# Two masked attention layers with residual layernorm: row stages rewritten, the first attention's ring and sums rearranged

## The chip, the cores and the metric

One core of one Trainium2 chip. The metric is device time in microseconds (us) of one launch. All inputs and outputs lie in HBM; the work that matters is done by TensorE (PE), VectorE (DVE), ScalarE (ACT), GpSimd (POOL) and the DMA queues that SyncE (SP), ACT and POOL issue.

## The reference, cut to what matters

```python
# N = 4096 nodes, 8 heads of 64, 512 features; adj is a 4096 x 4096 0/1 matrix (about 0.4% ones, diagonal set)
x_l     = (x @ W + b).reshape(N, 8, 64)
scores  = alpha_l[:, None, :] * alpha_r[None, :, :]      # alpha: x_l against att_l, att_r, per head
att     = softmax(where(adj > 0, scores, -9e15), axis=1)
x1      = layernorm(x + relu(einsum('ijh,jhc->ihc', att, x_l)))
scores  = einsum('hnd,hmd->hnm', x1 / 8, x2)             # second layer: x1 as queries, x2 as keys
attn    = softmax(where(adj > 0, scores, -9e15), axis=-1)
out     = layernorm(x1 + einsum('hnm,hmd->hnd', attn, v))
```

## The kernel before, in words

The kernel runs five stages one after the other, with a barrier of all engines between two of them.

1. `prepare` transposes the mask into SBUF as 0/1 bytes, computes `x_l` and the alphas, splits the keys `x2` into two fp16 parts, and writes them to scratch tensors in HBM. Its tail computes one shift per head (a bound on the scores, so that the exponential can't overflow) for the first attention, stores it, loads it back, and compares it with a limit. A branch then takes the plain way (`attend_gat`) or, for large bounds, another one (`attend_with_maximum`). For these inputs the plain way is taken.
2. `attend_gat` is the first attention. It has 16 groups (4 chunks of 1024 queries by 4 pairs of heads), and each group goes over 32 tiles of 128 source rows. Per tile and head ACT computes `exp(scale * al_bc + shift)` (line 515, 128x1024), DVE multiplies it by the mask (line 528), and PE multiplies the result by the values: `values`, line 544, 4 fp32 products per tile, each two matmul records. Masked weights live in a ring `w` of 5 tiles. They are also summed over source rows, for the softmax denominators, in one of two ways. The tiles not in `BY_DMA` (20 of 32) go through PE as products with ones (`denominators`, line 553), two tiles at a time (`COUPLES`); the 12 tiles in `BY_DMA` are added by DMAs with an accumulating write that POOL issues (lines 587 and 589, 1 MB each), in two chains into two totals; PE then multiplies both totals by ones after the fourth tile of the next group (`close`). A place of the ring is free again when its values are multiplied and its sum is done; ACT waits for both. The source rows `g_xl` come in blocks of 4 tiles into 2 places (line 469); SP waits until the block two before is multiplied.
3. `finish_layer` for layer 0 works on row tiles of 128 rows in rounds of four, in a hardware loop. PE transposes the attention's output (line 705: 4 fp32 products with the identity, 8 records), adds three products for rows without a neighbour (line 710), and transposes the denominators (lines 712 and 714). DVE takes the reciprocal (817), scales (819), applies relu and adds x (827; in layer 1 a plain add, 830), and gathers mean and variance (833, 836). After four tiles ACT takes the square root (749), DVE its reciprocal (838), and DVE normalizes the four tiles (842). In layer 0 PE then transposes the result again for the queries (721), ACT takes the upper fp16 part (757), DVE the lower (847). POOL meanwhile sums the rows of v (782), squares the result (786) for a bound on the query norms, DVE reduces the squares (850), and POOL stores the queries. The tail makes the second layer's shift out of the largest query norm and stores and reloads it (to line 870).
4. `attend_dot`, the second attention.
5. `finish_layer` for layer 1, without the query part.

The order of the work on each engine is the order in which its instructions are written; engines meet only through the semaphore counts in the code.

## Time and profile before

| | us |
|---|---|
| median of 3 runs | 3963.24 (3959.92 to 3971.84) |
| profiled execution, its own time | 3969.57 |
| its span (first to last instruction) | 3967.8 |
| granted TensorE clock, mean | 0.946 |

Busy over the span: PE 3642.8 us (92%), DVE 2993.9 (75%), ACT 2515.8 (63%), POOL 1649.9 (42%). The stages can be told by which line is at work: the first product of the first attention starts at 395.1 us, the first row stage at about 1791, the second attention's products at about 2002, the last row stage at about 3808. A busy share is an average over stages with different limits; what one stage costs is read in the window of that stage. Records of matmuls overlap, so the time from one start to the next is the cost of one in a dense stretch, not its own duration.

### The profile page before, as it was taken

What the parts mean: (1) busy time and instruction counts of PE and PEld (TensorE: products, weight loads), DVE (VectorE), ACT (ScalarE), POOL (GpSimd) and SP (SyncE); (2) the same over time, 40 slices, a digit from 0 to 9 for tenths busy, and PEclk for the clock granted to TensorE, in tenths of its full rate; (3) what the DMA queues carried; (4) which work ended last, traced back from release to release, by engine and by line L of the source; (5) the groups of instructions that cost most, each with busy time, mean ns of one, the idle gap of its engine ahead of it and who ended that gap; (6) DMA issues with size and microseconds to landing.
All of it is one profiled execution on the core that took longest, in us unless ns stands there. A gap on an engine that the chain in (4) does not pass through costs nothing. (4 is left out here: it accounts for less than half of the span.)

```text
span 3967.8 us, 59303 instructions
## 1 busy us (share of the span) xinstructions
PE 3642.8 (92%) x22662; PEld 1506.6 (38%) x22662; DVE 2993.9 (75%) x3014; ACT 2515.8 (63%) x2394; POOL 1649.9 (42%) x1258
## 2 busy tenths in 40 slices
PE   7887999999999998996689999999999999999977
PEld 4654222222222222224534444444444444444445
DVE  5555888888888888887867777777777777777756
ACT  3444888888888888881256666666666666656620
POOL 3333111111011111114556666776666767776620
PEclk9988999999999999995589999999999999999965
DMA  7886788888878888876589999999999999999954
GB/s 262 286 291 225 173 189 191 192 192 184 193 172 194 187 190 187 190 173 235 189 179 204 202 201 202 203 198 204 203 202 202 207 201 198 204 199 204 193 167 148
DMA packets 366770, 795.25 MB, mean 200 GB/s; under 512 B 31424, under 2 KB 203456, under 8 KB 341952
## 3 DMA queue, kind: packets, MB, share of 16 engines
q0 software_dynamic: 108544, 495.11, 61.5%
q1 hardware_dynamic: 240832, 271.41, 22.2%
q10 hardware_dynamic: 17152, 25.43, 1.8%
q8 instruction: 161, 2.64, 0.3%
q14 instruction: 81, 0.66, 0.0%
HBM read 262.70 MB, written 59.38 MB: 81 GB/s over the span
## 5 line engine op out<-in xcount | busy, mean ns | idle before, releaser
L1104 DVE TENSOR_TENSOR a_weights<-a_psS,maskT 128x1024 f32<-128x1024 f32 x1024 | 1206.1, 1220 | 461.8 <-ACT a_psS L1069 461.7
L1069 ACT ACTIVATE a_psS<-a_psS,a_shift 128x1024 f32<-128x1024 f32 x1024 | 1071.5, 1084 | 678.7 <-PE a_psS L997 678.6
L528 DVE TENSOR_TENSOR g_weights<-g_weights,maskT 128x1024 f32<-128x1024 f32 x1024 | 1178.0, 1220 | 220.1 <-ACT g_weights L515 219.1
L515 ACT ACTIVATE g_weights<-al_bc,g_shift,g_xl 128x1024 f32<-128x1024 f32 x1024 | 1178.0, 1230 | 158.4 <-DMA g_xl<-xl_scratch 70.3
L544 PE MATMUL g_psO<-g_weights,g_xl 128*64 128x512 f32 x4096 | 966.8, 605 | 128.8 <-DVE g_weights L528 126.9
L997 PE MATMUL a_psS<-a_q,a_k 128*64 128x512 f16 x8192 | 971.5, 380 | 19.3 <-DMA a_k<-k_scratch 17.8
L1014 PE MATMUL a_psO<-a_weights,a_v 128*64 128x512 f32 x4096 | 961.2, 592 | 0.0
L1127 POOL TENSOR_TENSOR a_pool_total<-a_pool_total,a_weights 128x1024 f32<-128x1024 f32 x336 | 915.9, 2726 | 0.0
L997 PEld LDWEIGHTS a_psS<-a_q,a_k 128*64 128x64 f16 x8192 | 463.3, 110 | 649.3 <-issue 300.2
L1135 POOL DMA_DIRECT2D a_dma_total<-a_weights x480 | 446.1, 929 | 409.8 <-DVE a_weights L1104 214.2
L544 PEld LDWEIGHTS g_psO<-g_weights,g_xl 128*64 128x64 f32 x4096 | 269.9, 137 | 819.4 <-issue 541.8
L589 POOL DMA_DIRECT2D g_total<-g_weights x160 | 137.2, 858 | 822.3 <-DVE g_weights L528 744.3
L1014 PEld LDWEIGHTS a_psO<-a_weights,a_v 128*64 128x64 f32 x4096 | 287.4, 137 | 393.7 <-issue 305.3
L553 PE MATMUL g_psD<-g_weights,onesF 128*32 128x512 f32 x2560 | 307.8, 598 | 0.0
L264 ACT ACTIVATE maskT<-psM 128x1024 bf16 x128 | 125.7, 1035 | 182.5 <-PE psM L284 181.9
L587 POOL DMA_DIRECT2D g_total<-g_weights x32 | 17.8, 557 | 418.0 <-PE g_psD L553 326.6
L239 POOL TENSOR_TENSOR xl_sum<-xl_sum,xl_sb 128x512 f32<-128x512 f32 x32 | 72.9, 2277 | 235.7 <-DVE xl_sb L376 235.7
L705 PE MATMUL f_psO<-identF,f_oT 128*128 128x128 f32 x512 | 122.3, 414 | 39.4 <-DMA f_oT<-o_scratch 21.4
L553 PEld LDWEIGHTS g_psD<-g_weights,onesF 128*32 128x32 f32 x2560 | 66.8, 109 | 225.8 <-issue 225.8
L749 ACT ACTIVATE f_std<-f_mv,f_eps 128x4 f32<-128x4 f32 x16 | 4.8, 297 | 232.9 <-DVE f_mv L836 232.9
L312 PE MATMUL psL<-w_sb,xT 128*128 128x512 f32 x256 | 134.4, 673 | 11.3 <-ACT xT L257 11.3
L1090 DVE TENSOR_TENSOR a_dve_total<-a_dve_total,a_weights 128x1024 f32<-128x1024 f32 x112 | 137.1, 1224 | 0.0
(129 smaller groups left out, 1774.5 us busy)
## 6 DMA issues: line engine op xcount, KB each, us to landing
a_dma_total<-a_weights POOLq DMA_DIRECT2D x512, 512.0 KB, 5.3
g_total<-g_weights POOLq DMA_DIRECT2D x192, 1024.0 KB, 7.9
adj_sb<-in_adj_dram SPq DMA_DIRECT2D x128, 512.0 KB, 6.0
g_xl<-xl_scratch SPq DMA_DIRECT2D x128, 260.0 KB, 4.7
a_k<-k_scratch SPq DMA_DIRECT2D x256, 128.0 KB, 5.4
a_v<-in_L_gnn_v_dram SPq DMA_DIRECT2D x128, 256.0 KB, 3.9
al_bc<-alpha_scratch SPq DMA_DIRECT2D x16, 1024.0 KB, 5.3
f_oT<-o_scratch SPq DMA_DIRECT2D x16, 1024.0 KB
```

The lines of the kernel that those rows point to most:

```text
L515: nc.scalar.activation(w[:, u % RING, h, :], al_bc[:, g % 2, h, :], ACT.Exp, bias=shift_bc[:, g % 2, h:h + 1], scale=xl[:, slot, u % KB, 2 ...
L528: nc.vector.tensor_tensor(w[:, u % RING, h, :], w[:, u % RING, h, :], maskT[:, j, (g // PAIRS) * IC:(g // PAIRS + 1) * IC], ALU.mult).then ...
L544: last = nc.tensor.matmul(psO[g % 2][h * C:(h + 1) * C, hf, :], xl[:, slot, u % KB, h * C:(h + 1) * C], w[:, u % RING, h, hf * HALF:(hf + ...
L553: ins = nc.tensor.matmul(psD[g % 2][row:row + 32, :], onesF[:, 0:32], weights[:, h, hf * HALF:(hf + 1) * HALF], start=first, stop=last)
L589: pool.dma_start(total[:, chain, :, :], w[:, u % RING, :, :], accum_op=ALU.add).then_inc(dma_added[chain], 16)
L997: last = nc.tensor.matmul(psS[n % RING][low:low + C, hf, :], k_sb[:, slot, h, keys:keys + C], q_sb[:, par, part, h, hf * HALF:(hf + 1) * H ...
L1014: last = nc.tensor.matmul(psO[h * C:(h + 1) * C, hf, :], v_sb[:, slot, u % KB, h * C:(h + 1) * C], w[:, u % NP, h, hf * HALF:(hf + 1) * HALF],
L1069: nc.scalar.activation(psS[n % RING][:], psS[n % RING][:], ACT.Exp, bias=shift_bc[:, g % 2, h:h + 1], scale=SCALE).then_inc(exped, 1)
L1090: nc.vector.tensor_tensor(dve_total[:], other, w[:, u % NP, 0, :], ALU.add).then_inc(dve_added, 1)
L1104: nc.vector.tensor_tensor(w[:, u % NP, h, :], psS[n % RING][:].rearrange("p a c -> p (a c)"), maskT[:, j, (g // PAIRS) * IC:(g // PAIRS + ...
L1127: pool.tensor_tensor(pool_total[:], other, w[:, u % NP, 0, :], ALU.add).then_inc(pool_added, 1)
L1135: pool.dma_start(dma_total[:, g % 2, chain, :], w[:, u % NP, 1, :], accum_op=ALU.add).then_inc(dma_added[chain], 16)
```

## The change

In `attend_gat` the ring has 6 places, `g_xl` 3, and the pattern of sums repeats every 8 tiles: tiles 1 and 5 of each 8 go by DMA in one chain into one total (8 of 32), the other six through PE as couples (0,2), (3,4), (6,7). The total is multiplied by ones at the end of the same group. POOL also adds the rows of v, two 256 KB accumulating transfers per group, into a sum that it stores at the end. SP stores the group before one block earlier.

In `prepare` the tail also computes the second layer's shift, from the largest key norm alone (a layernormed row has a squared norm of at most 512), with a square root on ACT; it stores `colsum`, the head mask and both shifts, and reloads both shifts.

In `finish_layer` the loop is written out; the steps of one tile are spread over steps of the loop (queries of tile t - 7 at step t); the fp32 transposes use the transpose mode; the three products for rows without a neighbour are one with 72 rows; normalizing moves from DVE to ACT; finding such rows moves from ACT to POOL; the sum of v, the squares and the reduction of norms are gone, and so is the reload of the shift at its end. Queries are stored in pairs of tiles by ACT. `attend_dot` is unchanged.

```diff
 # attend_gat
-        RING = 5
+        RING = 6
+        XS = 3
-        BY_DMA = (4, 6, 8, 11, 13, 15, 18, 20, 22, 25, 27, 29)
-        COUPLES = {second: (first, second) for first, second in zip(BY_PE[0::2], BY_PE[1::2])}
+        BY_DMA = (1, 5)
+        COUPLES = {2: (0, 2), 4: (3, 4), 7: (6, 7)}
-                if at >= 2:
-                    sp.wait_ge(multiplied, KB * (at - 1))
+                if at >= XS:
+                    sp.wait_ge(multiplied, KB * (at - XS + 1))
...
-                if j == LATE and g > 0:
-                    close(g - 1)
+                if j == NT - 1:
+                    pe.wait_ge(dma_added, 16 * added_by(g * NT + NT - JB + BY_DMA[-1]))
+                    denominators(g, total, last=True).then_inc(closed, 1)
...
+                if j in (3, 19):
+                    add_values(2 * g + j // 16)        # pool: v_sum += 128 rows of v, by DMA
...
 # prepare, tail
+            act.wait_ge(kmax_ready, 1)
+            nc.scalar.activation(reach[:], kmax[:], ACT.Sqrt, scale=F * SCALE * SCALE).then_inc(reach_ready, 1)
+            pool.wait_ge(tail_dve, 3)
+            pool.dma_start(col_dram[0], colsum[:]).then_inc(heads_stored, 16)
+            pool.dma_start(head_dram, headmask[:]).then_inc(heads_stored, 16)
+            for layer in range(2):
+                pool.dma_start(shift_dram[layer]..., shift[:, layer:layer + 1]).then_inc(shift_stored, 16)
+            pool.wait_ge(shift_stored, 32)
+            pool.dma_start(bounds[:], shift_dram[:, :]...).then_inc(shift_stored, 16)
...
 # finish_layer, PE
+                for a in range(PAIRS):
+                    nc.tensor.matmul(psO[t % 3][:, a * P:(a + 1) * P], oT[:, par, a, cols], identF[:], is_transpose=True,
+                                     start=(a == 0), stop=False, skip_group_check=True)
+                nc.tensor.matmul(psO[t % 3][:], alone[:, par, cols], colparts[:], start=False, stop=True,
+                                 skip_group_check=True)
 # finish_layer, ACT: one step per tile, t = 0 .. 38 (layer 0) or 32
+            for t in range(STEPS):
+                if t > 0 and t % T == 0 and t <= NT:
+                    normalize(t // T - 1)      # 4 Identity activations with scale and bias, then the store
+                if t < NT and t % T == T - 1:
+                    deviations(t // T)         # waits for the variance of tile t, square root
+                if first and t >= LAG:
+                    upper(t - LAG)
+                    if (t - LAG) % 2 == 0 and t > LAG:
+                        store_queries((t - LAG) // 2 - 1)
 # finish_layer, DVE
+            for t in range(STEPS):
+                if t < NT:
+                    divide(t)                  # reciprocal, scale
+                if t > 0 and t % T == 0 and t <= NT:
+                    deviate(t // T - 1)        # reciprocal of the root, offset
+                if t < NT:
+                    add(t)                     # add x, mean and variance
+                if first and t >= LAG:
+                    lower(t - LAG)
```

At the start of each row stage SP now loads `colsum` behind the first 1 MB of the attention's output, DVE makes three bf16 parts of it, and PE waits for them (`consts_set`, 9) before its first product; the denominators come three times, after POOL has cleared their tile.

## Rows read from the trace of the kernel before

**Rows 1.** Windows by stage: length, busy time (records) per engine, PEclk, DMA share, GB/s.

```profile
396.00:1791.00 1395.00, 1280.36 (x6912) 344.66 (x6908) 1174.63 (x1022) 1195.77 (x1052) 155.03 (x192) 0.99 0.81 186
1791.00:2002.00 211.00, 133.28 (x579) 99.63 (x579) 160.95 (x263) 36.56 (x57) 99.39 (x91) 0.57 0.63 208
2002.00:3805.00 1803.00, 1798.30 (x12544) 757.63 (x12544) 1345.66 (x1152) 1096.61 (x1057) 1265.09 (x864) 1.00 0.97 200
3805.00:3968.00 163.00, 117.25 (x448) 87.79 (x448) 98.41 (x207) 17.82 (x25) 0.00 (x0) 0.51 0.44 155
```

**Rows 2.** Waits in 396:1791, us in total, times, longest.

```profile
ACT g_weights L515 <- DMA g_xl<-xl_scratch: 54.8, 42, 2.9
ACT g_weights L515 <- PE g_psD L553: 41.1, 50, 2.0
ACT g_weights L515 <- DMA g_total<-g_weights: 40.8, 42, 2.5
```

**Rows 3.** Timeline of PE in a dense stretch: start, length, what, records.

```profile
894.00 7.30 PE L544 MATMUL g_psO<-g_weights,g_xl 128*64 128x512 f32 x32
901.23 1.92 PE L553 MATMUL g_psD<-g_weights,onesF 128*32 128x512 f32 x16
903.08 3.65 PE L544 MATMUL g_psO<-g_weights,g_xl 128*64 128x512 f32 x16
```

**Rows 4.** Timeline, first and last products of the first attention.

```profile
395.10 5.08 PE L544 MATMUL g_psO<-g_weights,g_xl 128*64 128x512 f32 x16 [19.05 <-DVE g_weights L528]
...
1784.21 1.90 PE L553 MATMUL g_psD<-g_total,onesF 128*32 128x512 f32 x16
```

**Rows 5.** DMAs: g_total's time to landing; g_xl's count, size, median time to landing.

```profile
DMA to landing us min/median/max: 4.4/7.9/12.3
g_xl<-xl_scratch SPq DMA_DIRECT2D x126, 260.0 KB, 4.7
```

**Rows 6.** Timeline of the first row stage: two reciprocals, one tile apart.

```profile
1826.90 0.17 DVE L817 RECIPROCAL f_rden<-f_psR 128x8 f32<-128x8 f32 x1
...
1829.50 0.18 DVE L817 RECIPROCAL f_rden<-f_psR 128x8 f32<-128x8 f32 x1
```

**Rows 7.** Instruction groups of 1792:1990: busy us, mean ns, idle before.

```profile
L847 DVE TENSOR_TENSOR f_ql<-f_psQ,f_qh 128x512 f16<-128x512 f32 x32 | 20.4, 680 | 0.3
L757 ACT ACTIVATE f_qh<-f_psQ 128x512 f16<-128x512 f32 x32 | 19.1, 598 | 29.1 <-PE f_psQ L721 29.1
```

**Rows 8.** Timeline: first reciprocal and last instruction of the first row stage.

```profile
1801.73 0.21 DVE L817 RECIPROCAL f_rden<-f_psR 128x8 f32<-128x8 f32 x1 [7.55 <-PE f_psR L714]
...
1990.11 0.14 DVE L870 TENSOR_SCALAR wide<-least 1x1 int32<-1x1 f32 x1
```

**Rows 9.** Timeline of the last row stage: one tile of PE, first reciprocal.

```profile
3818.30 2.08 PE L705 MATMUL f_psO<-identF,f_oT 128*128 128x128 f32 x8
3818.41 0.21 DVE L817 RECIPROCAL f_rden<-f_psR 128x8 f32<-128x8 f32 x1 [7.28 <-PE f_psR L714]
...
3820.31 1.46 PE L710 MATMUL f_psO<-f_colparts,f_alone 8*128 8x512 bf16 x3
...
3821.95 2.08 PE L705 MATMUL f_psO<-identF,f_oT 128*128 128x128 f32 x8
```

**Rows 10.** Timeline: four transposes in transpose mode; the reciprocal of the root.

```profile
1836.79 1.11 PE L721 MATMUL f_psQ<-identF,f_res 128*128 128x128 f32 x4 [4.50 <-DVE f_res L842]
...
1835.41 0.18 DVE L838 RECIPROCAL f_rstd<-f_std 128x4 f32<-128x4 f32 x1 [0.36 <-ACT f_std L749]
```

**Rows 11.** Groups of the whole span: table loads and activations of line 741.

```profile
L741 ACT ACT_TABLE_LOAD x8 | 10.3, 1283 | 30.6 <-DMA f_oT<-o_scratch 19.4 <-DVE f_res L842 9.7 <-issue 1.6
L741 ACT ACTIVATE f_alone<-f_dT 8x512 bf16<-8x512 f32 x16 | 9.9, 620 | 0.1
```

**Rows 12.** Timeline: the last store of the kernel is issued.

```profile
3963.06 0.38 ACTq L760 DMA_DIRECT2D out_dram<-f_res  x1
```

**Rows 13.** Timeline: the last instruction of the first stage.

```profile
382.29 0.14 DVE L400 TENSOR_SCALAR wide<-least 1x1 int32<-1x1 f32 x1
```

More of the change, by code:

```diff
@@ L435, in attend_gat @@
         summed = sem("g_summed")
-        dma_added = [sem(f"g_dma_added{i}") for i in range(2)]
+        dma_added = sem("g_dma_added")
         closed = sem("g_closed")
@@ L555, in denominators @@
                 return ins
-            def close(g):
-                for chain in range(2):
-                    pe.wait_ge(dma_added[chain], 16 * (g + 1) * (len(BY_DMA) // 2))
-                    ins = denominators(g, total[:, chain, :, :], last=(chain == 1))
-                ins.then_inc(closed, 1)
             for u in range(GROUPS * NT):
@@ L677, in wait_last @@
-        def wait_last(engine, counts, rr, par):
-            engine.wait_ge(counts[1 - par], (rr + par) * T)
+        STEPS = NT + LAG if first else NT + 1
         @block.sync
         def _(sp):
-            def load(r, rr, par):
-                rows = ds(r * (T * P), T * P)
-                sp.wait_ge(turned[par], rr * T)
-                sp.dma_start(dT[:, par, :], d_dram[layer, :, rows]).then_inc(o_loaded[par], 16)
+            for r in range(R):
+                par = r % 2
+                rows = slice(r * T * P, (r + 1) * T * P)
+                if r >= 2:
+                    sp.wait_ge(turned, T * (r - 1))
@@ new lines, in _ @@
+                for at in PARTS:
+                    sp.dma_start(dT[at:at + H, par, :], d_dram[layer, :, rows]).then_inc(d_loaded[par], 16)
+                if r >= 2:
+                    sp.wait_ge(added, T * (r - 1))
+                sp.dma_start(xin[:, par, :, :], x[rows, :].rearrange("(t p) c -> p t c", p=P)).then_inc(x_loaded[par], 16)
+            if first:
+                sp.dma_start(v_sum[:], vsum_dram).then_inc(v_loaded, 16)
+                sp.dma_start(headmask[:], head_dram).then_inc(v_loaded, 16)
+                sp.wait_ge(tail, 2)
+                sp.dma_start(col_dram[1], next_sum[:]).then_inc(tail, 16)
+                sp.wait_ge(tail, 18)
@@ new lines, in normalize @@
+            def normalize(r):
+                act.wait_ge(rstd_ready, r + 1)
+                act.wait_ge(offset_ready, r + 1)
+                for s in range(T):
+                    nc.scalar.activation(z[:, r % ZB, s, :], z[:, r % ZB, s, :], ACT.Identity,
+                                         bias=offset[:, r % 2, s:s + 1], scale=rstd[:, r % 2, s:s + 1]
+                                         ).then_inc(res_ready, 1)
+                act.wait_ge(res_ready, T * (r + 1))
+                act.dma_start(result[r * T * P:(r + 1) * T * P, :].rearrange("(t p) c -> p t c", p=P),
+                              z[:, r % ZB, :, :]).then_inc(res_stored[r % ZB], 16)
@@ new lines, in upper, with store_queries @@
+            def upper(t):
+                pair, half = divmod(t, 2)
+                act.wait_ge(q_turned, t + 1)
+                if half == 0 and pair >= 2:
+                    act.wait_ge(q_stored[pair % 2], 32 * (pair // 2))
+                nc.scalar.activation(qh[:, pair % 2, :, half * P:(half + 1) * P], psQ[t % 3][:], ACT.Copy
+                                     ).then_inc(qh_ready, 1)
+            def store_queries(pair):
+                act.wait_ge(ql_ready, 2 * pair + 2)
+                for part, qq in enumerate((qh, ql)):
+                    act.dma_start(q_dram[part].rearrange("(a p) n -> p a n", p=P)[:, :, pair * 2 * P:(pair + 1) * 2 * P],
+                                  qq[:, pair % 2, :, :]).then_inc(q_stored[pair % 2], 16)
@@ new lines, in lower @@
+            def lower(t):
+                pair, half = divmod(t, 2)
+                cols = slice(half * P, (half + 1) * P)
+                dve.wait_ge(qh_ready, t + 1)
+                if half == 0 and pair >= 2:
+                    dve.wait_ge(q_stored[pair % 2], 32 * (pair // 2))
+                nc.vector.tensor_tensor(ql[:, pair % 2, :, cols], psQ[t % 3][:], qh[:, pair % 2, :, cols],
+                                        ALU.subtract).then_inc(ql_ready, 1)
+            for t in range(STEPS):
+                if t < NT:
+                    divide(t)
+                if t > 0 and t % T == 0 and t <= NT:
+                    deviate(t // T - 1)
+                if t < NT:
+                    add(t)
+                if first and t >= LAG:
+                    lower(t - LAG)
@@ L1200, in attend_with_maximum, with _ @@
         ROUNDS = NT // ROUND
+        if layer == 0:
+            v_sum = sb("v_sum", [P, F], F32)
+            v_added = sem("v_added")
         block = ctx.enter_context(nc.Block())
+        if layer == 0:
+            @block.gpsimd
+            def _(pool):
+                for t in range(NT):
+                    rows = v[t * P:(t + 1) * P, :]
+                    if t == 0:
+                        pool.dma_start(v_sum[:], rows).then_inc(v_added, 16)
+                    else:
+                        pool.wait_ge(v_added, 16 * t)
+                        pool.dma_start(v_sum[:], rows, accum_op=ALU.add).then_inc(v_added, 16)
+                pool.wait_ge(v_added, 16 * NT)
+                pool.dma_start(vsum_dram, v_sum[:]).then_inc(v_added, 16)
+                pool.wait_ge(v_added, 16 * (NT + 1))
         def for_tiles(engine, work, new_head=None):
```

465 lines of the change are left out of this document (213 added, 252 removed).

## The prediction

> **What bounds the kernel now.** I read the windows by stage first, because a barrier separates the stages and each has its own limit. The second attention (1803 us) keeps PE busy for 1798.3 us [rows 1]; nothing in it is edited, and I leave it alone. The first attention lasts 1395 us with PE busy for 1280.4, ACT for 1195.8, DVE for 1174.6: nobody is full, so a wait between them sets the pace. The two row stages have PE busy for 133 of 211 us and 117 of 163 us, at a granted clock of 0.57 and 0.51 (1.2 GHz for most of it), and DVE for 161 and 98 us: chains there, not an engine.
>
> Next the waits of the first attention. ACT, the head of the chain, stops for source rows (54.8 us), for a place of the ring that PE still has to sum (41.1) and for one that a transfer still reads (40.8) [rows 2]: 136.7 us that it spends before it writes a weight. The time that would be left if they went is the longest engine's, and for that I need PE's true pace. In a dense stretch 32 records (four tiles of values) take 901.23 - 894.00 = 7.23 us, so 1.81 us a tile; 16 records of sums (two tiles) take 903.08 - 901.23 = 1.85, so 0.925 us a tile [rows 3]. PE before: 512 tiles x 1.81 = 927, plus 16 groups x (20 tiles + 2 totals) x 0.925 = 326, together 1253 us. Its first product starts at 395.1 and its last ends at 1786.1 [rows 4]: 1391 us, so 138 us are stalls, the same size as ACT's waits. ACT alone would need 1195.8 / 512 = 2.34 us a tile, its copies of results included, or 2.3 without them [rows 1].
>
> **First attention.** Sums: 24 tiles and 1 total per group through PE, three more units than before: 16 x 3 x 0.925 = +44 us of PE work. New PE floor: 927 + 16 x 25 x 0.925 = 927 + 370 = 1297 us, 2.50 us a tile on average, or 20.0 us per block of 8, above ACT's 2.3. Do the three waits of ACT go? I walk one block with PE never waiting, values of its tiles ending at 1.8, 3.6, 5.4 (couple done at 7.3), 9.1, 10.9 (12.8), 14.6, 16.4, 18.2 (20.0).
> - Ring: tile 0's place is free at 7.3 and belongs to tile 6. ACT writes it from 7.3 to 9.6, the mask is on one multiply later (1174.6 / 1022 = 1.15 us [rows 1]), with the hand-over at 10.9; PE wants it at 14.6. Cover 3.6 us. All other places are freed earlier relative to their need, the next tightest again at the next block's first couple.
> - Transfers: tile 9 (tile 1 of the next block) is masked at 17.7; its issue takes 155.0 / 192 = 0.8 us [rows 1] and it lands 7.9 us later on the median [rows 5], at 26.4; its place is wanted by ACT at 29.6. Cover 3 us, so a transfer may take up to 11 us unnoticed; before, with 5 places, a masked tile had 5 x 2.5 = 12.5 us until the mask of its successor, and 0.8 + 7.9 + 2.3 + 1.2 = 12.2 of them were used, hence the 42 waits. There are a third fewer of them, each 1 MB, so 7.9 is the likely upper side; the row's extremes are 4.4 and 12.3.
> - Source rows: with three places a block's load is issued when PE starts the block two before it, 20 us ahead of PE and 12 ahead of ACT, which leads PE by 8; it lands in 4.7 [rows 5]. The wait goes.
> - The close waits for tile 29's transfer: masked 13 us before PE reaches it, 8.7 used. What POOL has queued behind its waits is only the next transfer; the v transfers, 32 issues of under 1 us and 0.25 MB each, stand between two of those that are 10 us apart, and cost nothing as long as these 3 us of cover last. Between 0 and 32 x 1 = 32 us; I take 0.
> - What is late next is PE itself. ACT's two copies per group (about 1.6 us) eat into the cover of 3.6 and stay hidden.
>
> I add 8 us for the first block, where the filling of the ring sets the pace, and for leftovers: 1305 against 1391, **-86 us**. If the stalls all stayed it would be +44; if half stayed, -25.
>
> **Prepare's tail.** Key norm, square root, shift: ACT has to finish its own DMA issues, then load a table (1.28) [rows 11] and take a root; POOL issues four small stores instead of one, some 0.5 us each by the nearest row, an issue of 0.38 [rows 12], before the reload. I get 4 us on top of the 382.3 where it ended [rows 13], and another 1.3 because ACT has to load the exponential's table again: **+5 us** (3 to 9). The flag for the second layer: from the inputs the largest squared key norm is 126.4, so the bound is sqrt(512 x 126.4) / 8 = 31.8, under the limit of 38: the plain way is still taken.
>
> **Row stage, layer 1.** PE per tile before: 3821.95 - 3818.30 = 3.65 us [rows 9], the pace of the stage. Now: four transposes 1.11 at this low clock [rows 10] for 2.08, one product (about 0.49) for three (1.46), the rest as before: 3.65 - 0.95 - 0.97 = 1.75. DVE then sets the pace. Its five instructions on a tile take 1829.50 - 1826.90 = 2.60 us where nothing holds them [rows 6]. Per round of four one reciprocal and one small product, 0.4, since ACT's root is taken while DVE divides. 32 x 2.60 + 8 x 0.4 = 86.4 us. ACT's normalizing, by the nearest row 0.6 us a tile [rows 7], 2.5 a round of 10.8, lies beside it. Data: 24 MB in that time are 280 GB/s, which the first attention's 186 and this stage's 155 [rows 1] don't bound; I take it as hidden, at most +15.
>  Start: PE now waits for `colsum`, which queues behind 1 MB, and for DVE's 2.8 us chain of parts after it: first reciprocal 1.5 us later than at 3818.4 [rows 9] (0 to +4). End: from the last variance root 0.4, reciprocal and offset 0.4, four normalizings 2.5, issue and landing 4.7 (3963.06 to 3967.8, [rows 12]): 8.1.
>  3819.9 + 86.4 + 8.1 = 3914 against 3967.8: **-53 us** (-35 to -57).
>
> **Row stage, layer 0.** The same 2.60 and the lower part 0.69 [rows 7]: 3.29 per tile. Here I find two stalls in the order as written. At step 4r + 3 ACT stands at the wait for tile 4r + 3's variance, with `upper` queued behind it, and DVE's next is `lower`, which needs that `upper`: latency, root and copy, 0.06 + 0.30 + 0.60 + hand-overs = 1.1 us (the root's round trip to DVE is 0.36 [rows 10]). At step 4r + 4 ACT normalizes four tiles (2.6) and issues a store (0.4) before `upper` (0.6), DVE has 1.7 of other work after the offset: 2.0 us. A round is 13.2 + 0.4 + 3.1 = 16.7. PE, at 1.75 + 1.11 = 2.9 a tile, is under it. POOL's long adds, which stretched DVE's instructions, are gone. Seven tiles without queries 18.6, one of 4.4, six rounds 100.5, the last seven tiles' queries 12: 135.5 us from the first reciprocal, which comes at 1801.7 + 1.3 [rows 8]. Tail: sum of v through PE, its store, and the last query stores in parallel: about 5, then the barrier: 1943.5. Before, the last instruction was at 1990.1 [rows 8]: **-47 us** (-20 to -65). The ends: without the two stalls 22 us less; if ACT reloads tables (below), 20 more.
>
> **Sum.** +5 - 86 - 47 - 53 = -181 us. From the profiled execution's own 3969.6 this gives 3788.6; the median of the runs stands 6 us under that execution, so I say **3785 us**.
>
> **A rule weighed.** Line 741's Relu has 16 activations and 8 table loads [rows 11]: the second of each iteration, right behind the square root, needed none. The Trainium skill, "ScalarE: Activation LUTs", section "Table sets: the hidden batching unit", has identity and copy in every set, so that normalizing between two roots would load nothing; no trace here has an Identity, so this is open. The same page prices a switch at about 2.66 us with its drain. By its price two switches a round in 16 rounds would be 85 us of ACT, and by the row's 1.28 us 41.
>
> **The rivals.**
> - *The first attention keeps part of its stalls* (20%). For: three chains meet in one ring, and cover of 3 us is less than the spread of the landings (4.4 to 12.3). Against: one chain instead of two, fewer bytes. With half of the 138 us left: 1297 + 69 = 1366, so 3785 + 61 = 3846.
> - *ACT holds the row stages* (15%): Identity costs a table load and each root another. Layer 0: both stalls grow by 1.28, 8 rounds, +20; layer 1: the root comes 0.7 after DVE wants it, +5, and +3 at the end. 3785 + 28 = 3813. For: 8 loads each at 741 and 749 in the trace; against: the loads stand at the head of loop bodies only.
> - *More than I sum* (8%): no stalls in layer 0, a quicker tail: 3760.
> - *Slower* (3%): the single chain. Before, two chains of six could each take twice the time per transfer; now eight transfers follow one another per group, and each waits for the one before. If one with its issue takes over 20.0 / 2 = 10.0 us the chain sets the pace, and the kernel is slower once a group exceeds 87 + 95 / 16 = 93 us, at 11.6 us per transfer (95: what the other stages bring, less the tail). At 12.3 plus issue, 13.1, a group is 105: 16 x 105 + 3 = 1683 for 1391, 3963 + 292 - 95 = 4160. Against: the median of 7.9 was taken with two in flight.
>
> The forecast itself has 54%. The range reaches from 3755 to 3848. A measurement of this kernel tells about 0.3%, 12 us, from no change. Faster 0.96, within 0.02, slower 0.02 (the other 1% of the single chain would end inside 12 us).
>
> **What would show it.** First attention: about 81.5 us per group, PE idle under 1 us per group, ACT's waits now on PE and not on `g_xl`. Row stages: reciprocals 2.60 us apart in layer 1; in layer 0 two short waits of DVE's `lower` on ACT per round. One table load for roots per row stage. PE's clock still near 0.5 there. Wrong would be: waits of ACT on `g_total` or of POOL on its own chain; DVE idle on PE in layer 1; landings of `f_oT` over 15 us.

## The result, and the profile after

| | before | after |
|---|---|---|
| median of the runs, us | 3965.34 (4 runs, 3959.92 to 3971.84) | **3741.94** (4 runs, 3738.36 to 3745.04) |
| ratio, 95% interval | | 0.9436 (0.9418 to 0.9453) |
| profiled execution; its span | 3969.57; 3967.8 | 3745.04; 3743.1 |
| granted TensorE clock, mean | 0.946 | 0.957 |

The kernel became 5.6% faster, by 224 us. The forecast was 3785 with a range from 3755 to 3848: the direction held, and the time fell 13 us below the range's lower end. Split at the same events in both profiled executions (first and end of the last product of the first attention, first product of the second, end of the second's last copy of sums by ACT), in us:

| stage | before | after | difference | forecast |
|---|---|---|---|---|
| up to the first product of the first attention | 395.1 | 388.6 | -6.5 | +5 |
| first attention, first to last product | 1391.0 | 1280.5 | -110.5 | -86 |
| row stage, layer 0 | 216.4 | 165.7 | -51 | -47 |
| second attention | 1803.1 | 1803.1 | 0 | 0 |
| row stage, layer 1 | 162.2 | 105.3 | -57 | -53 |
| sum | | | -225 | -181 |

So 36 of the missed 44 us lie in two places, the first attention (24) and the first stage (12).

The windows by stage of the kernel after, columns as in [rows 1]: the first attention, and the two row stages.

```profile
388.00:1695.00 1307.00, 1292.11 (x7342) 369.95 (x7342) 1180.28 (x1051) 1185.54 (x1054) 138.01 (x164) 0.99 0.70 157
1700.00:1845.00 145.00, 89.74 (x380) 63.33 (x382) 92.36 (x187) 49.05 (x76) 8.82 (x8) 0.52 0.71 218
...
3640.00:3743.00 103.00, 70.10 (x256) 45.79 (x256) 81.51 (x185) 27.09 (x41) 13.28 (x9) 0.50 0.74 249
```

Against [rows 1] PE is busy for nearly all of the first attention, while ACT and DVE do what they did. In both row stages PE and DVE have less to do, at nearly the same low clock; POOL has less in layer 0, ACT more in layer 1, and POOL 13 us in layer 1 where it had none. (The attention's last product ends at 1669.1; the rest of the first window is the barrier and the first tiles of the row stage, and the second window begins behind them.)

The waits of the first attention, for [rows 2]. Before, PE waited for masked weights 181 times, which [rows 2] doesn't show:

```profile
PE g_psO L544 <- DVE g_weights L528: 126.9, 181, 19.1
```

After, the three stalls of ACT are one, and short:

```profile
DVE g_weights L538 <- ACT g_weights L525: 105.9, 79, 1.5
ACT g_weights L525 <- PE g_psD L563: 88.4, 64, 1.5
POOL g_total L602 <- DMA g_total<-g_weights: 67.7, 8, 9.3
PE g_psO L554 <- DVE g_weights L538: 23.2, 1, 23.2
```

ACT's weights wait for nothing but PE, and PE for DVE once, at the very start. The forecast had named waits of POOL on its own chain as a sign of being wrong, and there are eight, up to 9.3 us long; they cost nothing here, since no other engine's wait for `g_total` shows. One block of eight tiles on PE, for [rows 3]:

```profile
1037.33 3.65 PE L554 MATMUL g_psO<-g_weights,g_xl 128*64 128x512 f32 x16
1040.91 1.92 PE L563 MATMUL g_psD<-g_weights,onesF 128*32 128x512 f32 x16
1042.77 5.37 PE L554 MATMUL g_psO<-g_weights,g_xl 128*64 128x512 f32 x24
1048.07 1.92 PE L563 MATMUL g_psD<-g_weights,onesF 128*32 128x512 f32 x16
1049.92 5.37 PE L554 MATMUL g_psO<-g_weights,g_xl 128*64 128x512 f32 x24
1055.22 1.92 PE L563 MATMUL g_psD<-g_weights,onesF 128*32 128x512 f32 x16
1057.08 1.51 PE L554 MATMUL g_psO<-g_weights,g_xl 128*64 128x512 f32 x6
```

From start to start, 24 records (three tiles) take 5.30 us and 16 records (two tiles) 3.58: one tile more costs 1.72, and the rest, 0.14, is the switch to the sums. A block is 1057.08 - 1037.33 = 19.75 us. The sums split the same way, with the total at the end of a group behind a couple:

```profile
468.49 1.92 PE L563 MATMUL g_psD<-g_weights,onesF 128*32 128x512 f32 x16
470.23 1.04 PE L563 MATMUL g_psD<-g_total,onesF 128*32 128x512 f32 x8
471.20 5.37 PE L554 MATMUL g_psO<-g_weights,g_xl 128*64 128x512 f32 x24
```

Three units take 471.20 - 468.49 = 2.71 us where two take 1.85, so a unit costs 0.86 and the switch back 0.13. Four blocks and a total are 4 x 19.75 + 0.86 = 79.9 us, and 16 groups are 1278: the stage takes 2 to 3 us more than PE's own time. Nearly all of that is at the start, where the first three tiles take 8.09 us for 5.30.

The first waits of `lower` and one round of four tiles in the row stage of layer 0, on DVE (start, length, what, idle before), for [rows 6] and [rows 7]:

```profile
1707.78 0.69 DVE L882 TENSOR_TENSOR f_ql<-f_psQ,f_qh 128x512 f16<-128x512 f32 x1 [0.85 <-ACT f_qh L775]
1708.39 0.20 DVE L833 RECIPROCAL f_rden<-f_psR 128x8 f32<-128x8 f32 x1
...
1713.72 0.69 DVE L882 TENSOR_TENSOR f_ql<-f_psQ,f_qh 128x512 f16<-128x512 f32 x1 [2.48 <-ACT f_qh L775]
1714.33 0.20 DVE L833 RECIPROCAL f_rden<-f_psR 128x8 f32<-128x8 f32 x1
...
1724.55 0.20 DVE L833 RECIPROCAL f_rden<-f_psR 128x8 f32<-128x8 f32 x1
```

The two stalls stand where the forecast put them, 0.85 and 2.48 us for 1.1 and 2.0. A round is 1724.55 - 1708.39 = 16.2 us for 16.7. In layer 1 nothing holds DVE (reciprocals, and the end):

```profile
3651.72 0.21 DVE L833 RECIPROCAL f_rden<-f_psR 128x8 f32<-128x8 f32 x1 [2.34 <-PE f_psR L728]
...
3654.31 0.18 DVE L833 RECIPROCAL f_rden<-f_psR 128x8 f32<-128x8 f32 x1
...
3656.80 0.17 DVE L833 RECIPROCAL f_rden<-f_psR 128x8 f32<-128x8 f32 x1
...
3732.04 0.17 DVE L833 RECIPROCAL f_rden<-f_psR 128x8 f32<-128x8 f32 x1
...
3738.40 0.38 ACTq L767 DMA_DIRECT2D out_dram<-f_z  x1
```

### The profile page after: what moved, and what is told of

It is laid out like the page before. It is cut to its first block and busy times, and to the rows that moved or that the text cites. A ratio compares the mean times of both kernels' runs of the same rounds, so it can differ in the third digit from the quotient of the medians.

```text
span 3743.1 us, 58557 instructions
## 1 busy us (share of the span) xinstructions
PE 3551.1 (95%) x22661; PEld 1448.4 (39%) x22661; DVE 2909.1 (78%) x2948; ACT 2525.6 (67%) x2430; POOL 1569.5 (42%) x1157
## 5 line engine op out<-in xcount | busy, mean ns | idle before, releaser
L554 PE MATMUL g_psO<-g_weights,g_xl 128*64 128x512 f32 x4096 | 924.1, 598 | 23.2 <-DVE g_weights L538 23.2
L1161 POOL DMA_DIRECT2D a_dma_total<-a_weights x480 | 467.1, 973 | 399.6 <-DVE a_weights L1130 202.5
L602 POOL DMA_DIRECT2D g_total<-g_weights x112 | 95.8, 855 | 939.1 <-DVE g_weights L538 871.4
L563 PE MATMUL g_psD<-g_weights,onesF 128*32 128x512 f32 x3072 | 369.4, 598 | 0.0
L563 PEld LDWEIGHTS g_psD<-g_weights,onesF 128*32 128x32 f32 x3072 | 80.1, 109 | 270.7 <-issue 270.7
L295 PE MATMUL psM<-identB,mask_sb 128*128 128x128 bf16 x1024 | 74.1, 227 | 40.2 <-DVE mask_sb L369 40.2
L369 DVE TENSOR_SCALAR mask_sb<-adj_sb 128x1024 bf16<-128x1024 int32 x128 | 98.8, 831 | 4.6 <-DVE ext L397 4.1
L599 POOL DMA_DIRECT2D g_total<-g_weights x16 | 9.0, 565 | 213.0 <-DVE g_weights L538 213.0
```

What stands on the lines that cost most here:

```text
L554: last = nc.tensor.matmul(psO[g % 2][h * C:(h + 1) * C, hf, :], xl[:, slot, u % KB, h * C:(h + 1) * C], w[:, u % RING, h, hf * HALF:(hf + ...
L563: ins = nc.tensor.matmul(psD[g % 2][row:row + 32, :], onesF[:, 0:32], weights[:, h, hf * HALF:(hf + 1) * HALF], start=first, stop=last)
L1161: pool.dma_start(dma_total[:, g % 2, chain, :], w[:, u % NP, 1, :], accum_op=ALU.add).then_inc(dma_added[chain], 16)
```

## The experiments

All times are medians of the runs (range), with the ratio to the kernel before where it was timed beside it. "The changed kernel" is the one above; edits are against it unless said.

### The two halves

The kernel before with only the new first attention (no sum of v), and the changed kernel with only the old first attention (v summed in it).

```diff
 # e1_gat_only: the kernel before
-def attend_gat(...)      # old
+def attend_gat(...)      # new, without add_values
 # e2_rows_only: the changed kernel
-def attend_gat(...)      # new
+def attend_gat(...)      # old, with add_values and its final store
```

> The kernel before with only the new first attention (ring of six, three places, 2 of 8 tiles by one chain), without the sum of v there. Theory: first product to last product of that stage 1281 us as in the trace of after, against 1391: -110 us, so about 3965 - 110 = 3855 in all. Rival: part of the 110 comes from what surrounds it (the sum of v, the changed start): then 1290 or more.

> The kernel after with the old first attention (ring of five, two places, 12 of 32 tiles in two chains), with the sum of v by accumulating transfers in it. Theory: the row stages keep their gains of 51 and 57 us whatever stands ahead; the first attention is at 1391 plus what the 32 transfers cost it; in all 3965 - 108 - (0 to 10 in the first stage) + (0 to 10) = 3850 to 3862. Rival: the v transfers, queued on the engine that issues the chains, delay the ring of five, which has no cover: 1400 to 1420 us there.

Measured: 3853.32 us (3852.01 to 3854.24), ratio 0.9714 (0.9698 to 0.9730), and 3865.35 (3864.26 to 3868.56), 0.9746 (0.9730 to 0.9763). The halves bring -112 and -100 us, together 212 of 224. The second half's first attention, at 1401 us, lies at the edge of its rival's range (1400 to 1420), and the kernel 3 us over the theory's. The old first attention with the transfers of v takes 1401 us, first product to last, for 1391 without them: in the old order those 32 transfers cost about 10 us, in the new one none can be seen (1278 us from the start of the first product to that of the last without v, 1280 with v). The second half holds those 10 us against itself, so the halves add up.

### Which part of the ring's rearrangement pays

Single resources were taken back first.

```diff
 # e3_ring5
-        RING = 6
+        RING = 5
 # e5_xs2
-        XS = 3
+        XS = 2
 # e6_pattern_only: both of these
```

> The kernel after with a ring of five, all else kept. Theory: the sixth place is what gives the transfers cover. With five, tile 0's place is free at 7.3 us of a block and is wanted for tile 5 (masked by 10.9, needed by 12.8, cover 1.9), and a place that a transfer reads has 12.5 us for 12.2: PE waits 1 to 3 us per group, 1300 to 1330 us for the stage, +20 to +50 us. Rival: the regular pattern alone does it and five places are enough: within 5 us of after.

> The kernel after with two places of source rows, ring of six and the new pattern kept. Theory: the load of a block is issued 10 us ahead of PE and ACT leads PE by 8, so a landing of 6.7 us leaves ACT waiting some 3 to 5 us per block of four; its lead then shrinks until it matches, and PE waits little: 0 to 30 us in the stage, so 0 to +30 in all. Rival: three places are what removed the stalls: +50 or more.

> The kernel after with a ring of five and two places of source rows: of the changes to the first attention only the regular pattern with 8 of 32 tiles by one chain, and the close within the group, are left. With a ring of five alone the stage took 1284 us, 3 more than after. If the pattern carries the gain: 1285 to 1310 us in the stage. If the pattern needs one of the two covers: 1340 or more.

Measured: five places of weights 3747.57 (3745.16 to 3748.78), ratio 0.9449 (0.9434 to 0.9465); two places of source rows 3779.41 (3772.69 to 3781.31), 0.9523 (0.9507 to 0.9538); both together 3745.57 (3742.00 to 3747.43), 0.9440 (0.9424 to 0.9456). The theory for five places, +20 to +50 us, missed: it is +6. The last is the kernel after, within the intervals: **neither the sixth place nor the third place is needed, only the pattern.** But the sixth without the third costs 37 us. Waits of ACT in that kernel's first attention:

```profile
ACT g_weights L525 <- DMA g_xl<-xl_scratch: 81.4, 24, 6.3
```

Why is seen in where transfers and loads are issued. With six places (the kernel after), one load of source rows leaves just ahead of a transfer of 1 MB, and the next one 1.7 us behind a transfer:

```profile
728.77 0.37 SPq L479 DMA_DIRECT2D g_xl<-xl_scratch  x1
728.86 0.85 POOL L602 DMA_DIRECT2D g_total<-g_weights  x1 [9.33 <-DVE g_weights L538]
...
737.93 0.85 POOL L602 DMA_DIRECT2D g_total<-g_weights  x1 [8.22 <-DVE g_weights L538]
...
739.64 0.37 SPq L479 DMA_DIRECT2D g_xl<-xl_scratch  x1
```

The first of these two loads lands in 3.5 us, the second in 6.8:

```profile
DMA to landing us min/median/max: 3.5/3.5/3.5
...
DMA to landing us min/median/max: 6.8/6.8/6.8
```

With five and two places ACT and DVE run one tile less ahead, and the load leaves more than 2 us before the transfer:

```profile
738.35 0.37 SPq L479 DMA_DIRECT2D g_xl<-xl_scratch  x1
...
740.49 0.85 POOL L602 DMA_DIRECT2D g_total<-g_weights  x1 [9.81 <-DVE g_weights L538]
```

Size and median time to landing of the loads, in the kernel after and in the one with five and two places:

```profile
g_xl<-xl_scratch SPq DMA_DIRECT2D x128, 260.0 KB, 6.7
```

```profile
g_xl<-xl_scratch SPq DMA_DIRECT2D x128, 260.0 KB, 2.9
```

The median of 6.7 is a mixture. In the trace of the kernel after, between 470 and 1650 us, 59 loads leave 0.6 to 1.7 us behind a transfer and land in 6.7 to 8.8 us (median 7.1); the other 58 land in 2.8 to 5.0 (median 3.1). With five places, and two or three of rows, no load leaves less than 6 us behind a transfer. With six and two, 27 loads leave up to 1.6 us behind one and take 7.3 us at the median, up to 9.2, and ACT waits for source rows 24 times. So the third place hides a delay that the sixth brought.

The reverse question, the third place in the old order:

```diff
 # e8_places_only: e2_rows_only with
-        xl = sb("g_xl", [P, 2, KB, XW], F32)
+        xl = sb("g_xl", [P, 3, KB, XW], F32)
```

> The kernel after with the old first attention (ring of five, 12 of 32 tiles in two chains, close after the fourth tile of the next group) but three places of source rows. With two places that stage took 1402 us. Theory: only ACT's waits on source rows go (58 us of them in that trace), and the ring, whose old couples and transfers have no cover, turns most of it into other waits: 1350 to 1400 us. Rival: source rows were the cause: 1345 or less.

Measured: 3866.25 (3865.14 to 3868.35), ratio 0.9750 (0.9735 to 0.9764): nothing gained over 3865.35. ACT's waits for source rows (58.4 us) went, and those for transfers rose from 48.9 to 105.6. A wait that is taken away alone shows up at the next resource.

What of the pattern, then? The old order was changed step by step into the new one, with five places and two.

```diff
 # f1_old_8of32: e2_rows_only with
-        BY_DMA = (4, 6, 8, 11, 13, 15, 18, 20, 22, 25, 27, 29)
+        BY_DMA = (4, 8, 11, 15, 18, 22, 25, 29)
 # f2_regular_two: e2_rows_only with
+        BY_DMA = (1, 5, 9, 13, 17, 21, 25, 29)
-        LATE = 3
+        LATE = 0        # both totals closed after the first tile of the next group
```

> The changed kernel with the first attention of before (ring of five, two places of source rows, two chains, totals closed after the fourth tile of the next group), with one line altered: 8 of 32 tiles by transfers, at (4, 8, 11, 15, 18, 22, 25, 29), instead of 12. With 12 that kernel took 3865 us (first attention 1402); with the new pattern in the same places 3746 (1282). Theory A, fewer transfers is what counts (less collision with the loads of source rows, no place waits for a transfer): 3755 to 3775, first attention about 1295. Theory B, the regular spacing of sums through PE and the close in the same group count: 3830 to 3860, first attention 1365 to 1395, ACT's waits on PE's sums as before (41 us or more).

> As the run before it, but with the transfers at tiles 1, 5, 9, ..., 29, so that the couples are those of the change; still two chains into two totals, closed after the first tile of the next group, ring of five and two places of source rows. PE has one total per group more than in the change, 16 x 0.86 = 14 us. Theory A (number of transfers) and B (spacing) both give about 3760 with first attention 1295; the rival C, that one chain closed in its own group is what counts, gives 3800 or more. If the run before it is at 3830 or more and this one at 3760, the spacing is shown.

| first attention (ring 5, 2 places of rows) | time, us | PE's own time | stalls | kernel, median (range) | ratio |
|---|---|---|---|---|---|
| old order, 12 of 32 (e2) | 1401 | 1227 | 174 | 3865.35 | 0.9746 |
| old order, 8 of 32 (f1) | 1349 | 1290 | 59 | 3815.74 (3813.57 to 3820.47) | 0.9628 (0.9612 to 0.9644) |
| regular positions, two chains (f2) | 1306 | 1295 | 11 | 3770.74 (3769.84 to 3774.41) | 0.9513 (0.9497 to 0.9529) |
| one chain, closed in its group (e6) | 1281 | 1277 | 4 | 3745.57 | 0.9440 |

(PE's own time by the prices above, 1.72 per tile of values, 0.86 per unit of sums, 0.27 for each change to sums and back: 16 x (32 x 1.72 + 22 x 0.86 + 10 x 0.27) = 1227, with 26 units and 12 changes 1290, with 26 and 13 1295, with 25 and 12 1277. Time: start of the first product to start of the last.) Neither theory for 8 irregular ones held: 3816 us lies between their ranges, so each names a part. A third fewer transfers removes 115 us of stalls and adds 63 of PE work. Regular positions with the earlier close of the totals remove 48 and add 5; the two were changed together, and how much each brings is not shown (ACT's wait for the closed sums, before it copies them out, fell from 73.5 to 44.8 us in that step). The one chain removes 7 and saves 18 of PE. In the kernel with 8 irregular ones ACT's waits on transfers are nearly gone (2.6 us), but it still stops for sums and for source rows, which the irregular gaps leave late:

```profile
ACT g_weights L530 <- PE g_psD L568: 55.1, 60, 2.5
ACT g_weights L530 <- DMA g_xl<-xl_scratch: 28.0, 25, 2.7
```

### More by transfers

PE's own 1277 us could shrink if more sums left it. Once in one chain (three of eight), once in two chains with tiles summed singly where positions ask for it (the latter with the faster row stages of e10, below, so that 3720.16 is what it stands beside).

```diff
 # e9_chain12
-        BY_DMA = (1, 5)
-        COUPLES = {2: (0, 2), 4: (3, 4), 7: (6, 7)}
+        BY_DMA = (1, 3, 5)
+        COUPLES = {2: (0, 2), 4: (4,), 7: (6, 7)}
 # e11_both
+        RING = 5
+        BY_DMA = (1, 3, 5, 9, 11, 13, 17, 19, 21, 24, 26, 28)      # two chains, two totals
```

> The kernel after with tiles 1, 3 and 5 of each 8 by the one chain: 12 transfers of 1 MB per group instead of 8, each waiting for the one before. Theory, the point of the rival of the prediction that ends slower: the chain sets the pace once 12 x (issue and landing) exceeds PE's work, 12 x 8.2 = 98 us a group against 76; the stage 16 x 98 = 1575 us, in all about 4040, slower than before. Rival: a transfer alone on its queues lands in 5 us or less, and the stage stays under 1300.

> The same, with 12 of 32 tiles of the first attention by transfers again, but in two chains, ring of five, three places, and each tile for PE summed at once where its neighbour isn't. PE's work is 76 us a group and ACT's 75, against 79.9 now. Theory: a place read by a transfer must come free in 0.8 + 7.9 + 2.3 + 1.2 = 12.2 us per 5 tiles, 2.44 a tile or 78 us a group, 30 us less than after in the stage: about 3685 in all. Rival: more transfers in flight land later than 7.9 us and give it all back: 3715 or more.

Measured: 4012.37 us (one run), slower than before: the first attention takes 1548 us, 97 per group of 12 transfers, which is 8.1 us for each with its issue. POOL waits for its own chain, and ACT for POOL's transfers:

```profile
POOL g_total L602 <- DMA g_total<-g_weights: 908.2, 132, 8.9
...
ACT g_weights L525 <- DMA g_total<-g_weights: 292.6, 104, 5.7
```

That is the mechanism of the forecast's rival "slower", met at 12 transfers a group instead of eight. In two chains: 3747.99 (3744.72 to 3749.09), ratio 0.9449 (0.9437 to 0.9462), first attention 1307 us with ACT waiting 100 us on transfers (94 times), 26 us worse than with 8 of 32, although PE has some 24 us less to do (22 units and 16 changes: 1253). The theory of 3685 failed, and its rival held.

### The first stage

The forecast had the first stage 5 us longer; it became 6.5 shorter, and the loop that no line of the change touches ended sooner (last copy of the mask at 364.1 for 374.8). The change moved tensors in SBUF: `headmask`, `colsum` and four small ones no longer stand ahead of that loop's buffers. The kernel before was profiled again, and the changed kernel with the loop's buffers at their old addresses.

```diff
 # e4_old_place
+        sb("place0", [H, F], BF16)      # and place1 to place4, as large as the five tensors of before
         wide = sb("wide", [1, 2], I32)
...
-        headmask = sb("headmask", [H, F], F32)
-        colsum = sb("colsum", [H, F], F32)
         w_sb = sb("w_sb", [P, 5, F], F32)
...
         least = sb("least", [1, 2], F32)
+        headmask = sb("headmask", [H, F], F32)
+        colsum = sb("colsum", [H, F], F32)
```

> The kernel before, profiled once more, for the time of its first stage alone: the last mask copy of that stage ended at 374.8 us in the trace of before and at 364.1 in the trace of after, though the loop before it is not edited. Theory: this is a spread between executions, so this trace may show anything from 362 to 376. Rival: the change causes it (placement in memory), so this trace again shows 373 to 376. The other stages: 1391, 216, 1803 and 162 us, each within 3.

> The kernel after, with the tiles of the first stage put back to the SBUF addresses that they had before (five dummy tiles of the old sizes ahead of them; head mask and column sum allocated last). In the traces of before, its repeat and the first-attention-only kernel the last mask copy of the first stage ends at 372 to 375 us and ACT's two issues of alpha_scratch take 2.1 us a round; in after and its two relatives 359 to 364 and 1.05. Theory A: the place of the tiles in SBUF sets this, so this trace shows 372 to 375 and about 2.1 us. Theory B: it is something else (places in HBM, the longer tail, the length of the program), so it stays at 359 to 365 and 1.05.

Measured: before again 3965.24 us, last copy of the mask at 374.7; the changed kernel with the old addresses 3758.02, last copy at 374.8 (each one run; the runs of one kernel spread over 1 to 12 us). The 16 small stores of the alphas (instruction, count, duration in ns: shortest, median, longest) in the changed kernel, with the old addresses, and in the second profile of the kernel before:

```profile
L281 ACTq DMA_DIRECT2D alpha_scratch<-alphaT x16: 300/572/792, 65.0 to 365.7; - x16
```

```profile
L286 ACTq DMA_DIRECT2D alpha_scratch<-alphaT x16: 817/870/1123, 63.5 to 376.7; - x16
```

```profile
L273 ACTq DMA_DIRECT2D alpha_scratch<-alphaT x16: 822/864/1127, 65.2 to 376.6; - x16
```

With the addresses the old durations return, and the 11 us with them. What about the address makes an issue take 0.87 us or 0.57 stays open. ACT pays it on the loop's path. Its idle time at the loop's head contains these two issues, and is shorter in the changed kernel, as is its wait for PE's transposes of the mask; before, and after:

```profile
ACT maskT L264 <- PE psM L284: 181.9, 33, 10.4
ACT L257 <- issue: 17.3, 7, 2.5
```

```profile
ACT maskT L273 <- PE psM L295: 175.6, 33, 10.4
ACT L266 <- issue: 10.9, 7, 2.2
```

That is 6.4 and 6.3 us, against 1.2 of new waits for `k_scratch`: together the 11. With the old addresses the two waits are back at 17.3 and 181.7. How the later start of a round lengthens the wait for PE was not followed.

The start of the first attention has a scatter of its own, though: in the kernels with the changed first stage it lies between 383.7 and 390.4, and with the old one between 392.9 and 395.1. The changed kernel with the old addresses starts it later than all of them:

```profile
400.37 1.98 PE L559 MATMUL g_psO<-g_weights,g_xl 128*64 128x512 f32 x4 [24.28 <-DVE g_weights L543]
```

That is 5.3 us after the kernel before (395.1), where the forecast had +5 for the longer tail: with the addresses held, the first stage does what was forecast (one trace, of a kind that scatters by some 7 us).

### The row stage of layer 0

DVE's `lower` waits since ACT takes `upper` behind normalizing and behind the wait for the variance. In e7 ACT takes `upper` first. In e10, besides that, the query parts have three pairs of buffers, and ACT's own queue loads `colsum` and the first denominators, which stood behind 1 MB in SP's.

```diff
 # e7_upper_first
             for t in range(STEPS):
+                if first and t >= LAG:
+                    upper(t - LAG)
                 if t > 0 and t % T == 0 and t <= NT:
                     normalize(t // T - 1)
                 if t < NT and t % T == T - 1:
                     deviations(t // T)
-                if first and t >= LAG:
-                    upper(t - LAG)
 # e10_three_pairs, on top
-            qh = sb("qh", [P, 2, PAIRS, 2 * P], F16)       # and ql
+            qh = sb("qh", [P, 3, PAIRS, 2 * P], F16)
...
+            act.dma_start(colsum[:], col_dram[layer]).then_inc(c_loaded, 16)
+            for at in PARTS:
+                act.dma_start(dT[at:at + H, 0, :], d_dram[layer, :, 0:T * P]).then_inc(d_loaded[0], 16)
 # f3_pairs_small: e10 with
+        RING = 5
+        XS = 2
```

> The kernel after with ACT's order in the row stages changed: the upper part of the queries ahead of normalizing and ahead of the wait for the variance. In the trace of after DVE's lower part waits 0.85 us on ACT at one tile of a round and 2.4 us at the next. Theory: both waits go and DVE's work sets the pace, 8 rounds x 3.2 = 22 to 26 us less, about -0.6%. Rival: PE's chain (3.1 us a tile at the low clock, through its wait for the reciprocal) takes over, and the gain is 10 us or less.

> The kernel with ACT's order changed (upper part first), and in addition three buffers of query pairs instead of two, and at the start of each row stage colsum and the first denominators loaded by ACT's queue at once, not behind 1 MB. In the trace with the order alone ACT waited 39 us for its own query stores, so its gain was 11 and not 22. Theory: the third buffer gives back 8 to 12 us, the start 3 us per row stage: 3742 - 11 - 10 - 6 = 3715. Rival: the stores are bound by their small packets, so a third buffer only delays the wait: 3725.

> The best version so far (row stages with three query buffers, upper part first, first loads by ACT's queue: 3720 us) with ring of five and two places of source rows instead of six and three. Theory: the sixth place of weights and the third of source rows cancel, so 3718 to 3728. Rival: the two together are worth their 0.8 MB of SBUF once the row stages are short: 3735 or more.

Measured: e7 3731.18 us (3728.72 to 3732.50), ratio 0.9403 (0.9388 to 0.9419), row stage 11.6 us shorter. The 30 us of `lower`'s waits don't come back whole, since ACT now meets the stores of its own buffers, as do DVE's last waits:

```profile
ACT f_qh L775 <- DMA q_scratch<-f_ql: 39.1, 8, 6.9
...
DVE f_ql L882 <- ACT f_qh L775: 19.1, 11, 3.3
```

e10 takes that wait away: **3720.16 us (3715.62 to 3723.59), ratio 0.9383 (0.9370 to 0.9396)**, the fastest of all, its row stage 143 us for 166. The loads that ACT's queue issues early brought nothing: the first reciprocal comes 17.0 us after the attention's last product for 16.6 in the kernel after, because PE now waits for POOL's comparison (below), and layer 1 takes 106.1 us for 105.3. So the gain over e7 is the third buffer's; the 6 us that were expected of the start are missing. f3 has 3724.05 (3723.88 to 3725.15), 0.9393 (0.9377 to 0.9409): with the short row stages too, the sixth place and the third are worth nothing that can be told apart.

## Why the prediction was wrong, step by step

- **First attention, mechanism: right.** The three stalls went, PE became the bound and waits once, at the start, and the chain of transfers stayed hidden. ACT waits on PE instead, as said.
- **First attention, size: the step that failed.** The forecast's floor, 1297 us, rests on "1.81 us a tile" out of 7.23 us for four tiles [rows 3]. That dense-looking stretch still held a short pause. Another stretch of four tiles in the same trace has none:

```profile
407.40 7.09 PE L544 MATMUL g_psO<-g_weights,g_xl 128*64 128x512 f32 x32
414.42 1.92 PE L553 MATMUL g_psD<-g_weights,onesF 128*32 128x512 f32 x16
```

It takes 414.42 - 407.40 = 7.02 us, as four tiles at 1.72 and a switch of 0.14 do. The floor is 1278, 19 us lower; of the 8 us that I added for leftovers 2 to 3 came. Together 24. With the right price the stalls before were 1391 - 1227 = 164 us, not 138; that 138 came out as large as ACT's three waits (136.7) was chance, and looked like a confirmation. Two stretches of unequal length would have separated tile from switch and shown it; one stretch can't.
- **Each reason for the stalls' going: half right.** The walk through a block gave the sixth place 3.6 us of cover and the third place the end of ACT's wait for source rows. The runs with five and two places show that neither was needed: fewer transfers, regular positions and the single chain carry it all. The forecast took the three places for the cause of a gain that the order of the work brings. The transfers' landing was right (7.7 us at the median for 7.9); the loads' was taken at 4.7 [rows 5], and half of them came to about 7, which the third place hides.
- **First stage: wrong by 12 us.** The tail itself cost 10.4 us from the last mask copy to the verdict, 7.6 before; the table load and the four stores are in it, +4 with the exponential's reload, close to the +5. What was not in the sum is the loop's 11 us, an effect of addresses that no row of before could show; it is the second step that failed, a stage taken as unchanged up to its tail. Some 5 us of scatter of the stage lie on top of both.
- **Row stage, layer 0: right, 4 us off.** From the first reciprocal (1685.7) to the end of the last `lower` (1820.5) it takes 134.8 us for 135.5. First reciprocal one microsecond later against the last product than before, as said (1.3). The rest is the tail.
- **Row stage, layer 1: right, 4 us off.** The tile's price was again one that included something: 2.49 us for 2.60 between reciprocals [rows 6], and 32 x 0.11 = 3.5. The five instructions are as long as before; what shrank is the step from `f_stats` to `f_mv`, 0.73 us where it was 0.84. In the old code a semaphore increment of its own (`stats_seen`) stands between the two, in the new one none. That it is the cause was read from the code and not tried alone. With 0.4 per round for the root, 3732.04 - 3651.72 = 80.3 us for 31 tiles. ACT's normalizing took 0.73 us a tile (2.92 for four) for 0.6, and stayed beside it.
- **Table loads: right.** Two loads for the square root in both row stages, none for Identity between them. The Trainium skill, "ScalarE: Activation LUTs", section "Table sets: the hidden batching unit", has identity in every set: the trace agrees. The same page of the Trainium skill, section "What ACT_TABLE_LOAD costs", adds a drain of about 1.38 us to the load and comes to about 2.66 us for every switch; the rows have the load and no drain. The loads of both row stages in one group (busy us, mean ns, idle before),

```profile
L757 ACT ACT_TABLE_LOAD x2 | 2.6, 1283 | 49.4 <-DVE f_mv L874 49.4
```

on the timeline of the first stage's tail, where the next activation starts 0.02 us behind the load's end,

```profile
366.23 1.28 ACT L284 ACT_TABLE_LOAD   x1 [1.17 <-issue]
367.53 0.20 ACT L284 ACTIVATE reach<-kmax 8x1 f32<-8x1 f32 x1
```

and in the kernel before, where a load starts 0.02 us behind the end of an activation:

```profile
1844.39 0.63 ACT L741 ACTIVATE f_alone<-f_dT 8x512 bf16<-8x512 f32 x1
1845.04 1.28 ACT L749 ACT_TABLE_LOAD   x1
```

- **The range.** Its lower end stood 30 us under the forecast and allowed only for the row stages' stalls and tail. The two prices taken from one stretch each, of PE in the first attention and of DVE in the row stages, had no bound from below; with the floor at 1278 the forecast itself would have been about 3766 and the lower end under 3742. A slip of the sum is in it too: 3788.6 less the 6 us is 3782.6, not 3785, and 2.4 us of the miss are that.

## What to carry to other kernels

Take the price of an instruction in a mix from the difference of two stretches of different length; a single "dense" stretch hides short pauses and the cost of switching in it, and 5% of a stage that one engine bounds is tens of microseconds. Where several chains (engine, transfer, load) meet in one ring, first make their positions repeat and thin out the slowest, and only then add places: here fewer transfers, the order and the single chain brought all 110 us, the sixth and the third place together brought nothing, and the sixth alone cost 37. Where a small load and a large transfer are in flight at once, look which of them left first. When a stage that nobody edited gets faster or slower, look at the durations of its DMA issues and at where its buffers lie now.

## What the hardware showed unexpectedly

- The issue of one and the same small store from ACT takes 0.87 or 0.57 us at the median; in the changed kernel the SBUF addresses of the buffers were the only thing altered between the two (the three rows above).
- A 260 KB load lands in about 3 us when it leaves ahead of a 1 MB accumulating transfer, even by 0.1 us, and in about 7 when it leaves 0.6 to 1.7 us behind one.
- A chain of such transfers that bounds the stage sustains one per 8.1 us, issue included (97 us for 12); eight in a group of 80 us had one each 10 us and cost nothing.
- POOL's comparison of 72x512 values takes 1.6 us on the mean and 1.88 the first time; in e10 PE's first transpose waits for it, and it for the landing of the denominators.
